# A graph-transformer layer on one core: two edge passes replaced by one pass over rows of one node and eight edges, with a merge

## The reference, cut to what matters

```python
e = jnp.einsum('ehd,ehd->eh', k[src], q[dst]) / jnp.sqrt(jnp.float32(H * D))
emax = jax.ops.segment_max(e, dst, num_segments=N)
ex = jnp.exp(e - emax[dst])
denom = jax.ops.segment_sum(ex, dst, num_segments=N)
a = ex / denom[dst]
m = v[src] * a[..., None]
ft2 = jax.ops.segment_sum(m, dst, num_segments=N).reshape(N, F)
```

## Time and profile before

| | us |
|---|---|
| median of 3 runs | 3281.3 (3278.27 to 3283.2) |
| span of the profiled execution | 3285.7 |
| busy: TensorE, GpSimd, VectorE, ScalarE | 2477.2, 1859.6, 1741.0, 931.8 |

### The profile page before, as it was taken

How to read it: one execution, slowest core, us unless ns; L and a number is a source line. 1 busy time by engine, 2 the same in 40 slices (tenths; PEclk the granted TensorE clock), 3 DMA queues, 4 the chain that set the end, 5 groups by cost and what they waited for, 6 DMA issues and landing times. The chain is left out here.

```text
span 3285.7 us, 55786 instructions
## 1 busy us (share of the span) xinstructions
PE 2477.2 (75%) x14138; PEld 2022.6 (62%) x14139; DVE 1741.0 (53%) x3705; ACT 931.8 (28%) x1985; POOL 1859.6 (57%) x1845
## 2 busy tenths in 40 slices
PE   2568778777777773099888888778869960999996
PEld 1446555555555552088777677666758850888885
DVE  3357666666656655277555555555538982121121
ACT  0235444444444440122111111111115520222221
POOL 1447767777767676667777777777740007122222
PEclk9888888888878785599888887888869985999998
DMA  3657666666666665443333333333333004566664
GB/s 108 176 137 171 167 157 161 160 160 160 164 154 159 152 159 134 124 122 97 97 101 99 98 101 98 96 100 97 96 105 127 0 27 135 173 191 193 200 188 128
DMA packets 232673, 433.09 MB, mean 132 GB/s; under 512 B 39575, under 2 KB 138678, under 8 KB 231950
## 3 DMA queue, kind: packets, MB, share of 16 engines
q0 software_dynamic: 94384, 230.02, 29.3%
q1 hardware_dynamic: 129275, 193.06, 18.0%
q10 hardware_dynamic: 8882, 8.62, 0.9%
HBM read 379.07 MB, written 46.46 MB: 130 GB/s over the span
## 5 line engine op out<-in xcount | busy, mean ns | idle before, releaser
L635 POOL DMA_INDIRECT v_ring<-v_tab,v_idx x808 | 881.9, 1091 | 262.7 <-issue 226.9
L635 POOL DMA_INDIRECT k_ring<-k_tab,k_idx x808 | 770.8, 954 | 324.8 <-issue 216.9
L1324 PE MATMUL sum_ps<-xn_buf 128*125 128x260 f32 x1808 | 560.9, 464 | 117.3 <-DVE xn_buf L1187 117.0
L1324 PEld LDWEIGHTS sum_ps<-xn_buf 128*125 128x125 f32 x1808 | 391.7, 228 | 203.3 <-DVE xn_buf L1187 131.5
L779 DVE TENSOR_TENSOR prod<-k_ring,q_ps 128x1024 f32<-128x1024 f32 x226 | 275.4, 1218 | 344.0 <-POOLq L641 295.8
L893 PE MATMUL q_ps<-q,spread 125*128 x2712 | 402.7, 307 | 48.8 <-DVE prod L779 24.8
L1187 DVE TENSOR_TENSOR xn_buf<-v_ring,e_all 128x1024 f32 x226 | 280.5, 1241 | 248.6 <-POOLq L641 248.5
L893 PEld LDWEIGHTS q_ps<-q,spread 125*128 125x128 bf16 x2712 | 290.4, 109 | 164.6 <-issue 95.8
L937 PE MATMUL sums_ps<-v,phi 125*124 125x33 f32 x1600 | 226.6, 289 | 117.5 <-DVE g_acc L794 71.0
L1898 POOL DMA_INDIRECT x_sum<-e_yw,to x64 | 99.7, 1557 | 379.6 <-DVE e_yw L1933 205.7
L937 PEld LDWEIGHTS sums_ps<-v,phi 125*124 125x124 f32 x1600 | 217.5, 212 | 147.7 <-issue 101.5
(11 more groups left out here) (289 smaller groups left out, 3219.5 us busy)
## 6 DMA issues: line engine op xcount, KB each, us to landing
e_w<-L_ffn_W SPq DMA_DIRECT2D x64, 1024.0 KB, 5.4
dst_row<-dst_pad SPq DMA_DIRECT2D x226, 250.0 KB
k_ring<-k_tab,k_idx POOLq DMA_INDIRECT x808
v_ring<-v_tab,v_idx POOLq DMA_INDIRECT x808, 2.8
x_rows<-v_ring SPq DMA_DIRECT2D x16, 516.0 KB
xr<-x_rows SPq DMA_DIRECT2D x32, 258.0 KB, 5.5
e_b<-L_ffn_b SPq DMA_DIRECT2D x32, 128.0 KB, 5.6
x_buf<-x ACTq DMA_DIRECT2D x5, 625.0 KB
```

The source lines that it names most:

```text
L635: pool.indirect_dma_start(out=self.ring[:, slot, j, :], out_offset=None, in_=self.table, in_offset=bass.IndirectOffsetOnAxis(ap=self.idx[h ...
L1324: mm = pe.matmul(sum_ps[c % 2][:, :], hot[c % 2][:, e, :], val[c % 2][:, e, :], start=(e == 0), stop=(e == EJ - 1))
```

## The change

The two edge passes and the softmax stage between them go. One stage, `stage_edges_and_mix`, takes their place, and a stage `stage_merge` follows it.

- Tiles are now 128 rows; a row is one node and up to eight consecutive edges (slots) from a block of eight; a block that reaches into the next node gives a row to each. There are 126 such tiles (TILES). A table `t3` of the edge blocks is written to DRAM by `stage_project`. For each tile SP loads 128 table rows and 128 q rows; VectorE compares, three small matmuls (`find`) place the rows, VectorE writes the indices, a 0/1 matrix and a mask (`settle`), four tiles ahead (AHEAD).
- k and v lie in one table; GpSimd issues eight indirect DMAs per tile, each 128 rows of 2 KB, into a ring of four tiles. One float32 matmul gives the q row of each table row, and VectorE multiplies it with all eight k slots.
- Scores, the maximum over the row's slots, the exponential and the weighted values are made at once. VectorE weights six slots, ScalarE two (`weigh_last`, eight activations of 64 columns). TensorE adds the eight slots up by eight 260-column matmuls with the identity; ScalarE copies the row sums out and they are stored to DRAM (`parts`), 130 KB per tile.
- The mixer's nine steps per window are cut to the order of `micro_steps`: four per tile, first the k half (micro steps 0 to 233), then the coefficients, then the q half (236 to 469). All of this stage is unrolled, without loops in registers.
- `stage_merge` finds the maximum of each node over its rows by scans, and then runs 150 steps of (tile, window): GpSimd rescales a tile's row sums (128x260), VectorE makes a 0/1 matrix, one matmul sums rows into nodes, VectorE adds it to the accumulator.
- `stage_project` makes k, v and q in one pass over the windows, unrolled, and q is no longer split into bf16 parts. The `Unit` takes its root as Ln and Exp on ScalarE, and the reciprocal on VectorE goes.

```diff
+L = 8
+NB = -(-EDGES // L)
+NBP = -(-NB // 128)
+TILES = -(-(NB - 1 + N) // 128)
+N_STEPS = TILES + NT - 1
...
+AHEAD = 4
+RING = 4
...
+def micro_steps(n, c):
+
+    i = 4 * n + c
+    if i < COEF_MICRO:
+        u, k = divmod(i, 9)
+        return [("k", u - 1, k)]
+    out = [("coef", 0, i - COEF_MICRO)] if i < COEF_MICRO + HM + 2 else []
+    u, k = divmod(i - Q_MICRO, 9)
+    if 0 <= u <= NT:
+        out.append(("q", u - 1, k))
+    elif u > NT:
+        out.append(("end", 0, i - Q_MICRO - 9 * (NT + 1)))
+    return out
...
+            for n in range(TILES):
+                pool.wait_ge(idx_ready, n + 1)
+                wait(pool, val_ready, 2 * (n - RING + 1))
+                wait(pool, act_val_ready, n - RING + 1)
+                pool.sem_inc(carrier, 1)
+                for e in range(L):
+                    pool.indirect_dma_start(out=ring[:, n % RING, e, :], out_offset=None, in_=t.kv_tab,
+                                            in_offset=bass.IndirectOffsetOnAxis(ap=idx[n % 6][:, e:e + 1], axis=0)
+                                            ).then_inc(landed[n % RING * 2 + e // (L // 2)], 16)
...
+            def compare(n):
...
+                dve.tensor_scalar(later[n % 2][:, :], t.iota[:, :], float(128 * n), blocks[n % 3][:, LAST:LAST + 1],
+                                  ALU.add, ALU.is_ge).then_inc(compared, 1)
...
+            def settle(n):
...
+                dve.tensor_scalar(t.nneg[:, n + 1:n + 2], where_ps[:, 2 * L:2 * L + 1], t.pcol[:, :], float(128 * n),
+                                  ALU.subtract, ALU.subtract).then_inc(placed, 1)
+                dve.tensor_copy(idx[n % 6][:, :], where_ps[:, 0:L]).then_inc(idx_ready, 1)
+                dve.scalar_tensor_tensor(spread[n % 6][:, :], local_ps, t.pcol[:, :], t.iota[:, :], ALU.add, ALU.is_equal
+                                         ).then_inc(spread_ready, 1)
+                dve.wait_ge(placed, n + 1)
+                dve.tensor_scalar(foreign[n % 6][:, :], where_ps[:, L:2 * L], t.nneg[:, n + 1:n + 2], 0.0, ALU.add, ALU.not_equal
+                                  ).then_inc(find_read, 1)
...
+            def times_q(n, half):
...
+                dve.tensor_tensor(prod[half][:, :, :], ring[:, n % RING, at, 0:F], bcast(q_ps[:, 0:F].unsqueeze(1), 128, L // 2, F),
+                                  ALU.mult).then_inc(q_read, 1)
...
+            def weigh(n, half):
+                at = slice(half * L // 2, (half + 1) * L // 2 - 1)
+                dve.wait_ge(exp_ready, n + 1)
+                dve.tensor_tensor(val[n % 2][:, at, :, 0:DG], ring[:, n % RING, at, F:2 * F].rearrange("p s (h d) -> p s h d", h=HG),
+                                  bcast(val[n % 2][:, at, :, DG:DG + 1], 128, L // 2 - 1, HG, DG), ALU.mult).then_inc(val_ready, 1)
...
+            def weigh_last(n):
...
+                for e in (L // 2 - 1, L - 1):
+                    for h in range(HG):
+                        one = act.activation(val[n % 2][:, e, h, 0:DG], ring[:, n % RING, e, F + h * DG:F + (h + 1) * DG], ACT.Copy,
+                                             scale=val[n % 2][:, e, h, DG:DG + 1])
+                one.then_inc(act_val_ready, 1)
...
+            def find(n):
...
+                pe.matmul(where_ps, t.ones[0:1, :], blocks[n % 3][0:1, 0:2 * L + 1], start=True, stop=False)
+                pe.matmul(where_ps, later[n % 2][:, :], blocks[n % 3][:, PREV:PREV + 2 * L + 1], start=False, stop=True)
+                pe.matmul(local_ps, t.ones[:, :], later[n % 2][:, :], start=True, stop=True).then_inc(found, 1)
...
+            def q_of_rows(n):
...
+                pe.matmul(q_ps[:, 0:F], spread[n % 6][:, :], q_win[n % 3][:, :], start=True, stop=True).then_inc(q_ready, 1)
...
+            def sum_rows(n, half):
...
+                for e in range(half * L // 2, (half + 1) * L // 2):
+                    mm = pe.matmul(rows_ps, t.ident[:, :], val[n % 2][:, e, :, :].rearrange("p h d -> p (h d)"),
+                                   start=(e == 0), stop=(e == L - 1))
+                if half:
+                    mm.then_inc(sum_ready, 1)
...
+            for n in range(TILES + 1):
+                for c in range(4):
+                    mix_first(n, c)
+                    if c == 1 and n + 1 < TILES:
+                        q_of_rows(n + 1)
+                    if c >= 2 and n > 0:
+                        sum_rows(n - 1, c - 2)
+                    if c == 3 and n + AHEAD + 1 < TILES:
+                        find(n + AHEAD + 1)
+                    mix_last(n, c)
...
+            for n in range(N_STEPS):
+                g = load_step(pool, t.step_g, n, TILES - 1)
...
+                pool.tensor_tensor(scaled[n % 2][:, :].rearrange("p (h d) -> p h d", h=HG),
+                                   loaded[:, ds(g & (MR - 1), 1), :].rearrange("p o (h d) -> p (o h) d", h=HG),
+                                   bcast(w_all[:, ds(g, 1), :].rearrange("p o h -> p (o h)").unsqueeze(2), 128, HG, DG + 1),
+                                   ALU.mult).then_inc(scaled_ready, 1)
...
+            def mark(n):
...
+                dve.tensor_scalar(hot[n % 2][:, :], t.iota_n[:, ds(w * TP, TP)], t.nneg[:, ds(g + 1, 1)], 0.0, ALU.add, ALU.is_equal
+                                  ).then_inc(hot_ready, 1)
...
+            for n in range(N_STEPS):
...
+                at = t.acc[:, old, :]
+                dve.tensor_tensor(at, at, step_ps[n % 2][:, 0:FD], ALU.add).then_inc(step_read, 1)
```

More of the change, by code:

```diff
@@ new lines, in late, with sums @@
+            def late(u, kind):
+                wait(pe, late_read, u * 2 + kind)
+                cols = slice(0, 2 * F) if kind == 0 else slice(2 * F, 3 * F)
+                for b in range(FC):
+                    mm = pe.matmul(late_ps[:, 0:cols.stop - cols.start], t.xnT[:, u, b * TP:(b + 1) * TP], t.w_late[:, b, cols],
+                                   start=(b == 0), stop=(b == FC - 1))
+                mm.then_inc(late_ready, 1)
+            def sums(u, kind):
+                wait(pe, slv_read, u * 3 + kind)
+                wait(pe, g_read, u * HM + 3 * kind)
+                parts = 1 if kind == 2 else 128
+                for half in range(2):
+                    lhsT = (t.ones[0:TP, 0:1] if kind == 2 else
+                            (ksq[u % 2] if kind == 0 else k_.unit[u % 2])[:, half * 128:(half + 1) * 128])
+                    mm = pe.matmul(slv_ps[0:parts, half, :], lhsT, v1[u % 2][:, 4 * half:4 * half + 4, :].rearrange("p h e -> p (h e)"),
+                                   start=True, stop=True)
+                mm.then_inc(slv_ready, 1)
```

1720 lines of the change are left out of this document (805 added, 915 removed).

## The result

The kernel before took 3282.3 us (3278.3 to 3290.3), the changed one 3201.1 us (3198.5 to 3203.9). The ratio is 0.9747, 95% interval 0.9732 to 0.9762; in a second set of runs 0.9753. It is 2.5% faster, where 2905 us, 11.5%, were forecast: the sign was right, the size wrong by 296 us, and the time lies outside of the stated range of 2750 to 3110. The profiled execution has a span of 3196.6 us.

The account below looks back on a forecast made before the run. GpSimd's count of indirect DMAs was taken to bound the old kernel. First product 196 + edge stage 1587 + last tile 12 + merge 267 + rest 847 = 2909 us span, 2905 us timed; range 2750 to 3110.

Parts of the forecast that it names:

- What sets the pace: Edge stage after the change: TensorE sets 12.8 us per tile, over 85% busy; GpSimd needs 10.9 us per tile.
- the rival that it costs by bytes: Gathers of 2 KB rows cost GpSimd by bytes: 17.9 us per tile, 3573 us in all; chance 0.05.
- I take 0.92: Edge stage: TensorE's granted clock assumed at 0.92, read from idle shares, giving 10.15 / 0.92 + 1.3 = 12.3 us per tile.
- the 10.15 us of work: Edge stage: TensorE's work per tile at full clock, 11.45 us less about 1.3 idle.
- a clock under 0.84: Edge stage: a sign that the prediction is wrong, which expected a clock of 0.9.
- The forecast of the edge stage, 1587 us: 112.5 tiles with mixer work, 1440 us, plus 13.5 tiles with little of it at GpSimd's 10.9, 147 us.
- The front: Loading and projection up to the edge stage: projection ends at 160 us, first product at 196, 5 later than before.
- the edge loads hold the first window up some 15: Projection: the edge loads delay its first window by some 15 us.
- 1.5 us per step: Merge: VectorE sets 1.5 us in each of 150 steps, 225 us; the whole merge 267 us.
- the rival that put it at 4.1: Merge at GpSimd's pace: multiplication 4.1 us, step 4.7, 480 us more, 3385 us in all; chance 0.04.
- The rival of the chain: Edge stage: each micro step costs the slower of VectorE and TensorE, 14 to 15 us per tile; chance 0.22.
- Full clock: Edge stage: TensorE stays at full clock and nothing meets badly, 11.45 us per tile, 2753 us in all; chance 0.12.

## Why the prediction was wrong

*What sets the pace: right.* TensorE is 90 to 92% busy in the edge stage and GpSimd's eight gathers at 0.96 + 0.30 are 10.1 of a tile's 14.8 us. The gather's price was right, 0.96 us for 2 KB rows as for 1 KB rows, and with it the rival that it costs by bytes is gone. The Trainium skill, "DMA: Bandwidth & Descriptors" (Why a DMA increments its semaphore by 16 and not by 1), has one descriptor per contiguous run. The equal price of both rows fits that; no record here counts descriptors.

*The tile: the steps that failed are "I take 0.92" and, a little less, the 10.15 us of work under it.* The edge stage ran at 0.82; the prediction itself had named a clock under 0.84 as a sign of its being wrong. The forecast's 12.8 us was 10.15 / 0.92 + 1.3 + 0.5. Measured, as a mean of both halves: 13.4 us busy, 1.3 idle. Busy time times granted clock is 664.44 x 0.85 / 50 = 11.3 in the k half and 10.8 in the q half, and in the kernel with find moved 11.1 and 10.7, so some 11.0 us of full-clock work per tile is an estimate that holds in four windows. The clock makes 10.15 / 0.825 - 10.15 / 0.92 = 1.3 us of the miss, the work (0.9 us more than I had counted from its bursts, at this clock) 1.1; the waits were 0.5 less than taken. That is 1.95 us x 112.5 tiles = 219; the tiles with little mixer work came out some 18 under the 147 us. A part of the missing work is `find`, which I took as three times 0.2 us: its three matmuls last 0.39, 0.40 and 0.47 us in the k half, 1.03 together since they overlap, at a clock of 0.85.

I had read the clock off the idle share, from two windows of the earlier trace rows. Idle share and clock of the windows now known: 23%, 0.84 and 16%, 0.84 (first and second pass before); 10%, 0.85 and 8%, 0.80 (changed); 8%, 0.90 and 4%, 0.88 (find moved); 10%, 0.73 and 5%, 0.55 (half the sums). The clock neither rises nor falls along with the idle share. Two points were too few, and two that contradicted them were in my own rows: 0.99 with 25% idle in ten us, and 0.84 with 23% in the whole first pass.

*What the clock does follow* is settled only in part. Shown, in one kernel: with four matmuls of 260 columns fewer per tile the clock fell from 0.85 and 0.80 to 0.73 and 0.55, and that cost as much as the matmuls had in the k half and more in the q half. With find moved out of the step that is already full into the one that stands, the clock rose to 0.90 and 0.88 on the first chip, and 70% of the stage's gain there is busy time and not idle time; on the slower chips the same move raised it by 0.01 and 0.02. Not shown: which property of TensorE's work it is. Covering the same wait by another route (pair sums ahead) left the clock as it was, and filling waits with added matmuls moved it by 0.03 at most against the kernels of the slower chips. The Trainium skill, "TensorE: Matmul & The Clock Gate" (What's actually happening), has the clock gated down by default and released by activity. The run with half the sums agrees in direction, less work and 0.80 to 0.55; that TensorE's busy share rose at the same time, from 92 to 95%, does not.

*The forecast of the edge stage, 1587 us, is nearly what the stage takes with find moved: 1601.* That is luck and no credit to the working: its parts are 0.89 of clock and 11 us of work instead of 0.92 and 10.15, with less waiting.

*The front: the term "the edge loads hold the first window up some 15" was 61.* That is 46 of the 69 us. Nothing was wrong in the order of the work; I priced the loads by their bytes and did not look at their partition count. The Trainium skill, "DMA: Bandwidth & Descriptors" (the same section), says that a transfer is given the largest number of engines up to 16 that divides the slowest dimension of both its sides, and that 127 partitions put all on one. The trace agrees: a DMA share of 0.06 at 26 GB/s, and 0.77 once the count is 112 and 15. The other 23 us: the projection ends at 235 us and not at 160, which is 29 beside the wait, and the way from there to the first product takes 29 us where 36 were taken. In the projection VectorE waits twelve times, 41 us in all, for the store of the normalised rows (`xn_dram`), and counting the blocks costs it seven times 5.4 us and not 4; for the first the forecast has no term. Its own terms (20 less, 25 windows at 3.0 to 3.5, 28, 15) add up to 165 to 177 us and not to 160, unless some of the 28 is hidden, which it does not say.

*The merge: 1.5 us per step was 1.69,* because two register loads leave 0.99 us and not 0.83 and the compare is 0.31 and not 0.25. That is 28 us; the way into the steps was some 7 shorter than taken. GpSimd's multiplication is 0.62 us, so the rival that put it at 4.1 falls. My estimate from the Trainium skill, "GPSIMD Engine Reference" (3.1 Elementwise), was 0.72; in bare proportion its 4497 ns for 2048 give 0.57 for 260, and the measured value lies between.

*The rival of the chain* (14.5 us per tile, 3096) came nearest by its number and is not what happened: in fifty tiles of the k half TensorE waits 25 us for VectorE's weighting, 19 for its additions and 23 for ScalarE, 76 of 740 us in all, and VectorE itself has 32% free. The pair sums ahead show that the additions stand next in line: with the wait for ScalarE gone, they took 17 of its 23 us. *Full clock* did not happen in any run.

## What to carry to other kernels

Where TensorE sets the pace, price its stretch at two clocks and ask which of them the new order of its work will be granted; an idle share does not tell. An ablation that removes matmuls can come out slower; what they cost is then read from busy time times granted clock and not from the total. Try spreading small matmuls into the steps that wait before building buffers that remove the wait: here the first went with 185 us in the stage on the first chip and gave 57 on a slower one, the second 3. Before pricing a load by its bytes, look at its partition count: 127 partitions went at 26 GB/s here, a DMA share of 0.06.

## What the runs showed of the hardware

*Less work, slower.* Leaving out four of a tile's matmuls took the granted clock from 0.80 to 0.55 and the kernel from 3199 to 3293 us.

*Slower chips, one stage.* On slower chip 1 the changed kernel's edge stage takes 2274 us and not 1786, at 0.71 to 0.75 of the clock and with TensorE idle 19 to 22% of the time instead of 8 to 10; VectorE's, ScalarE's and GpSimd's instructions last what they did, and the rest of the kernel takes the same time to within 4 us. The kernel before loses more there, 19%, so the ratio is better (0.945 and not 0.975); no trace of it on such a chip was taken. The timeline of the kernel with the split loads (chip 10) shows what the idle time looks like:
```profile
911.88 0.38 PE L1047 MATMUL bank_f<-pair,u_T 96*125 96x496 bf16 x1
...
914.38 0.94 POOL L663 DMA_INDIRECT ring<-kv_tab,idx  x1 [0.30 <-issue]
915.63 0.95 POOL L663 DMA_INDIRECT ring<-kv_tab,idx  x1 [0.30 <-issue]
916.87 0.58 ACT L966 ACTIVATE phi<-bank_f 125x496 f32<-125x496 f32 x1 [4.66 <-remote]
...
917.51 1.86 PE L1058 MATMUL bank_g<-v,phi 125*124 125x33 f32 x8 [4.80 <-issue]
```
The pair sums are over by their record at 912.3 us, ScalarE's square of them starts at 916.9, and GpSimd goes on meanwhile at its 1.25 us. ScalarE has 48 such waits of some 5 us in the k half of that kernel (247 us), on the first chip the changed kernel has none. No record names what stands still in them, and the cause is open.
